# Biases as a weight row, casts and copies on ScalarE, maxima over two heads at once, in a fused transformer and mixture-of-experts kernel

## The chip, the cores and the metric

The kernel runs on one core of a Trainium2 chip. The metric is the time on the device, in microseconds, from the first to the last instruction of one launch, with what lies around it. TensorE does the matmuls and transposes, VectorE and ScalarE read their results out of PSUM, GpSimd does elementwise work in SBUF, and SyncE issues the DMAs.

## What is computed

The input is 32 sequences of 256 token ids. Width is 192, with 12 heads of 16.

1. An embedding with a position table and a layer norm.
2. Four layers of windowed attention and a feed-forward part, on 32 sequences of 256 tokens:

```
q, k, v = heads(h @ Wq + bq), heads(h @ Wk + bk), heads(h @ Wv + bv)
scores  = q k^T / sqrt(16), only for |i - j| <= 64 and unmasked keys, else -1e9
h = layer_norm(h + softmax(scores) v @ Wo + bo)
h = layer_norm(h + gelu(h @ W1 + b1) @ W2 + b2)
```

3. One causal layer: a layer norm, q/k/v with a bias from `b_attn`, rotary embedding of q and k, causal softmax attention, a projection, a second norm.
4. A mixture of experts on the second norm's result: a shared expert, sigmoid scores of 16 experts, each expert's choice of 1024 tokens, and their weighted outputs added.

## The kernel before, in words

Four parts run one after another: `embed`, `tower` (the four token layers, then the causal layer), `choose` (which tokens each expert takes) and `experts`. The change touches `tower` alone.

**Tiles.** A sequence is 256 tokens, two tiles of 128 partitions. Two sequences, the sets s = 0 and 1, are in flight. Each set has four PSUM banks of 128 x 512 f32, `bank[s][0..3]`. q and k are held as bf16 stacks `[hi, lo, ...]` (`stack`, six slices of 16 per head, padded to 128), so that a bf16 matmul of two stacks gives f32-like products; a DMA transposes the stacks into `qkT`.

**Halves.** Every engine walks the same list of halves (`token_layers` L1041, `causal_layer` L1060). In one half, four sequences at different stages are worked on, called G, V, F and K. G and F are of one set, V and K of the other:

- G: hidden states transposed (`pe_hidden_T`, L439), copied to `hTa` by ScalarE (L683), q/k matmuls (`pe_qk`, L446), bias added by VectorE (`dve_qk`, L782), in the causal layer the rotation (`rotary`, L803: tile 0 on GpSimd, tile 1 on VectorE), then the stack (`dve_stack`, L817).
- V: value matmuls (`pe_v`, L459), bias added by VectorE into `vaug` (`dve_v`, L792); SyncE issues the transposes of the stack.
- F: first pass of scores, for the row maxima (`pe_scores1`, L471, in banks 0 to 2 in turn; `dve_row_max`, L838, one head each); the maxima are rounded (`dve_maxima`, L850), transposed (`pe_maxima`, L487) and copied as extra rows of `qkT` (`dve_maxima_rows`, L860).
- K: second pass of scores (`pe_scores2`, L499), exponents by ScalarE (L673), products with the values (`pe_products`, L515), transposes back (L554), division (att, L887, in the token layers with L898), transposes of att (L435), projection (`pe_project`, L562), residual (L945) and norm giving h1 (token layers L768 and L778; causal layer L756 and L760 into `xr`), transposes of h1 (L435), up projection (L582, causal L612), activation, down projection (L594, causal L627), residual and second norm (token layers). The unkept keys' share (`pe_unkept`, L537) exists in the token layers alone.

There are 128 full halves in the token layers and 35 halves in the causal layer, of which 29 have both G and K.

**Order.** There is no scheduler: each engine's program order is the order in `tensor_half` (L632), `scalar_half` (L665), `vector_half` (L912) and `pool_half` (L1008), and semaphores hold an engine until what it needs is done. TensorE interleaves second-pass head i with first-pass head i - 4, with product groups after i = 6, 10 and 13, then runs the rest in a fixed row: hidden_T, unkept, output transposes, maxima, att_T, values, project, q/k, h1_T, up, down. VectorE runs: row maxima, `dve_maxima`, sums and division, maxima rows, values, residual and norm to h1, q/k, (causal: sigmoid and gated products, rotation of tile 1), stack, and last the residual and second norm. GpSimd in a causal half: residual plus bias and rstd of the input norm of F, rstd1 of K (L1022), then a wait for the first q/k tile of G and four rotation instructions (L807, L810, L813, L815). This is the last:

```python
            if K:
                s = K.s
                ph.wait(pool, "var1", s, K.it)
                ph.inc(nc.gpsimd.tensor_tensor(rstd[s][:], ve[s][:], half[:], ALU.pow), "rstd1", s)
            if G and causal:
                s = G.s
                ph.wait(pool, "qk", s, G.it, 1)
                rc = Chain(ph, pool, G, "rot")
                rotary(nc.gpsimd, rc.link, s, 0)
```

Of the kernel before, what the change touches and what calls it, by code (L numbers as in the profile page):

```python
# [26 lines left out]
P = 128  # L27
D = 192
# [30 lines left out]
TOK_STACK_LINKS = 3  # L59
# [286 lines left out]
def tower(nc, a, hbuf, am_d, xs, sd, out, B, L):  # L346
# [4 lines left out]
    with ExitStack() as ctx:  # L351
# [5 lines left out]
        bank = [[ctx.enter_context(nc.psum_tensor(f"bank{s}{i}", [P, 512], F32)) for i in range(4)] for s in ST]  # L357


        wqk = sb("wqk", [DC, 2, 2 * D], F32)  # L360
        wv = sb("wv", [DC, 2, D], F32)
# [3 lines left out]
        vqk = sb("vqk", [P, 2 * D], F32)  # L365
        vv = sb("vv", [P, D], F32)
# [18 lines left out]
        hTa = sbs("hTa", [DC, 2, S], F32)  # L385
# [9 lines left out]
        mx = sbs("mx", [P, T, NH], F32)  # L395
        mrow = sbs("mrow", [P, T, NH, 32], BF16)
# [23 lines left out]
            sc1=NH, mx=NH, m=1, mT_ps=3, mT=3, sc2=NH, p=NH, pv=NH, ot=1, otT_ps=2, att=1,  # L420
# [18 lines left out]
        def pe_hidden_T(ph, pe, G, F, causal):  # L439
            s = G.s  # L440
            if F:
                ph.wait(pe, "y" if causal else "r2", F.s, F.it, 0)
            ph.wait(pe, "x0" if causal else "h_in", s, G.it)
            ph.inc(pe_transposes((h1 if causal else hcur)[s], bank[s][3]), "hT_ps", s)

        def pe_qk(ph, pe, G, F):  # L446
# [6 lines left out]
            for t in range(T):  # L453
                for c in range(2):
                    last = nc.tensor.matmul(bank[s][t][:, 0:2 * D], hTa[s][:, c, t * P:(t + 1) * P],  # L455
                                            wqk[:, c, :], start=(c == 0), stop=(c == 1))
                ph.inc(last, "qk_ps", s)

        def pe_v(ph, pe, V, G):  # L459
# [5 lines left out]
            for t in range(T):  # L465
                for c in range(2):
                    last = nc.tensor.matmul(bank[1 - s][3][:, t * D:(t + 1) * D], hTa[s][:, c, t * P:(t + 1) * P],
                                            wv[:, c, :], start=(c == 0), stop=(c == 1))
            ph.inc(last, "v_ps", s)

        def pe_scores1(ph, pe, F, h, masks, qcols, causal):  # L471
# [6 lines left out]
            if h >= 3:  # L478
                ph.wait(pe, "mx", s, F.it, h - 2)
            dst = bank[s][h % 3]  # L480
# [6 lines left out]
        def pe_maxima(ph, pe, F):  # L487
# [3 lines left out]
            for f in range(3):  # L491
                dst = bank[s][f][:].bitcast(BF16)
# [6 lines left out]
        def pe_scores2(ph, pe, K, V, h, masks, kcols):  # L499

            s = K.s
            if h == 0 and V:
                ph.wait(pe, "qk", V.s, V.it)
            if h == 0:
# [10 lines left out]
        def pe_products(ph, pe, K, F, g, kcols):  # L515
# [4 lines left out]
            if g == 2 and F:  # L520
                ph.wait(pe, "v", F.s, F.it)
# [110 lines left out]
        def tensor_half(ph, pe, G, V, F, K):  # L632
            causal = ph is not tok
            qcols, kcols, masks = (CAUSAL_Q, CAUSAL_K, 2) if causal else (BAND_COLS, BAND_COLS, 0)
            for i in range(NH + LEAD):
                if K and i < NH:
                    pe_scores2(ph, pe, K, V, i, masks, kcols)
                if F and i >= LEAD:
                    pe_scores1(ph, pe, F, i - LEAD, masks, qcols, causal)
                if K and i in PLAN.prod:  # L640
                    pe_products(ph, pe, K, F, PLAN.prod.index(i), kcols)
# [22 lines left out]

# [1136 lines left out]
```

## Time and profile before

| | us |
|---|---|
| median of 3 runs | 7051.08 |
| lowest, highest | 7049.91, 7069.48 |
| the profiled execution | 7050.01 |
| its span | 7048.2 |
| TensorE busy | 6042.4 (86% of the span) |
| VectorE busy | 4250.6 (60%) |
| ScalarE busy | 2239.1 (32%) |
| GpSimd busy | 1101.6 (16%) |

The mean granted TensorE clock is 0.939 of full speed; it has two levels, 2.4 GHz (1.0) and 1.2 GHz (0.5). Lines such as L435 are lines of the kernel before. "Idle before, releaser" is time in which an engine did nothing ahead of the instruction and what ended it. The chain of work that ended last covers only the last part of the span, the experts, so it says nothing about the changed part. To read the changed part, one has to look at the waits and at one half in order of time.

### The profile page before, as it was taken

What the parts mean: (1) busy time and instruction counts of PE and PEld (TensorE: products, weight loads), DVE (VectorE), ACT (ScalarE), POOL (GpSimd) and SP (SyncE); (2) the same over time, 40 slices, a digit from 0 to 9 for tenths busy, and PEclk for the clock granted to TensorE, in tenths of its full rate; (3) what the DMA queues carried; (4) which work ended last, traced back from release to release, by engine and by line L of the source; (5) the groups of instructions that cost most, each with busy time, mean ns of one, the idle gap of its engine ahead of it and who ended that gap; (6) DMA issues with size and microseconds to landing.
All of it is one profiled execution on the core that took longest, in us unless ns stands there. A gap on an engine that the chain in (4) does not pass through costs nothing. (4 is left out here: it accounts for less than half of the span.)

```text
span 7048.2 us, 128877 instructions
## 1 busy us (share of the span) xinstructions
PE 6042.4 (86%) x46786; PEld 4744.2 (67%) x46786; DVE 4250.6 (60%) x11172; ACT 2239.1 (32%) x4196; POOL 1101.6 (16%) x1089
## 2 busy tenths in 40 slices
PE   1999999999999999999999999978888883289999
PEld 0777777777777777777777777756666662266766
DVE  6666666666666666666666666666666664722222
ACT  0333333333333333334333333323333330011111
POOL 5011111111111111111111111111111110234333
PEclk9999999999999999999999999989999986699999
DMA  6322223323232322222332232332222320033322
GB/s 119 62 60 60 60 61 65 70 61 66 58 64 60 75 61 60 60 60 60 67 70 61 62 65 60 65 69 56 62 64 63 64 56 10 1 84 73 88 69 55
DMA packets 1204450, 441.09 MB, mean 63 GB/s; under 512 B 1050338, under 2 KB 1191044, under 8 KB 1204324
## 3 DMA queue, kind: packets, MB, share of 16 engines
q1 hardware_dynamic: 1176676, 402.69, 26.7%
q0 software_dynamic: 27648, 36.72, 3.4%
q8 instruction: 79, 1.29, 0.1%
q14 instruction: 47, 0.39, 0.0%
HBM read 124.23 MB, written 60.26 MB: 26 GB/s over the span
## 5 line engine op out<-in xcount | busy, mean ns | idle before, releaser
L673 ACT ACTIVATE pT<-bank 128x384 f32<-128x384 f32 x1920 | 907.9, 490 | 872.8 <-PE bank L511 872.8
L843 DVE TENSOR_REDUCE mx<-bank 128x2 f32<-128x384 f32 x1548 | 802.2, 554 | 322.0 <-PE bank L483 285.1
L582 PE MATMUL bank<-hT,w 96*128 96x256 f32 x3072 | 848.0, 442 | 85.9 <-ACT hT L688 85.9
L582 PEld LDWEIGHTS bank<-hT,w 96*128 96x128 f32 x3072 | 678.6, 224 | 236.2 <-ACT hT L688 118.2
L509 PE MATMUL bank<-maskb,eyeb 128*128 128x384 bf16 x1920 | 635.1, 331 | 78.6 <-ACT pT L673 73.3
L481 PE MATMUL bank<-maskb,eyeb 128*128 128x384 bf16 x1932 | 634.5, 328 | 39.9 <-DMA qkT<-stack 20.7
L483 PE MATMUL bank<-qkT 128*128 128x192 bf16 (+2 forms) x3864 | 636.5, 247 | 0.0
L511 PE MATMUL bank<-qkT 128*128 128x192 bf16 (+2 forms) x3840 | 630.9, 246 | 0.0
L993 DVE TENSOR_TENSOR hout<-bank,resid 128x384 f32<-128x384 f32 x128 | 71.3, 557 | 769.4 <-PE bank L594 769.4
L594 PE MATMUL bank<-w,pT 128*128 128x192 f32 x3072 | 520.4, 326 | 0.0
L1022 POOL TENSOR_TENSOR rstd<-ve,half 128x2 f32<-128x2 f32 x160 | 127.7, 798 | 2486.6 <-DVE ve L749 2486.6
L594 PEld LDWEIGHTS bank<-w,pT 128*128 128x128 f32 x3072 | 506.5, 190 | 6.6
L511 PEld LDWEIGHTS bank<-qkT 128*128 128x128 bf16 x3840 | 376.7, 98 | 136.9 <-issue 0.5
L483 PEld LDWEIGHTS bank<-qkT 128*128 128x128 bf16 x3864 | 379.4, 98 | 127.4 <-issue 2.2
L1709 PE MATMUL ps_g<-exp_xT,exp_wg 64*128 64x512 f32 x1152 | 456.6, 600 | 3.8 <-issue 3.1
L1709 PE MATMUL ps_u<-exp_xT,exp_wu 64*128 64x512 f32 x1152 | 446.7, 592 | 8.6 <-DMA emb_emb<-in_emb_word,emb_ids 7.3
L455 PE MATMUL bank<-wqk,hTa 96*128 96x384 f32 x1304 | 452.3, 490 | 1.4 <-ACT hTa L683 1.4
L531 PE MATMUL bank<-pT,vaug 128*32 128x192 f32 (+3 forms) x10752 | 413.5, 284 | 0.6 <-ACT pT L673 0.6
L688 ACT COPY hT<-bank 96x512 f32<-96x512 f32 x160 | 93.1, 582 | 1009.5 <-PE bank L435 1009.5
L701 ACT ACTIVATE pT<-bank,b 128x256 f32<-128x256 f32 x768 | 317.7, 472 | 294.1 <-PE bank L582 292.6
L1653 DVE TENSOR_TENSOR exp_hid<-exp_sg,ps_u 128x512 f32<-128x512 f32 x192 | 132.0, 687 | 429.5 <-PE ps_u L1709 368.5
L531 PEld LDWEIGHTS bank<-pT,vaug 128*32 128x32 f32 x10752 | 284.2, 109 | 117.6 <-issue 75.3
(197 smaller groups left out, 10230.5 us busy)
## 6 DMA issues: line engine op xcount, KB each, us to landing
hcur<-hbuf SPq DMA_DIRECT2D x165, 192.0 KB, 2.4
hbuf<-hout SPq DMA_DIRECT2D x128, 192.0 KB, 2.0
amb<-am_d SPq DMA_DIRECT2D x131, 128.0 KB, 2.9
exp_wg<-in_ewg SPq DMA_DIRECT2D x16, 768.0 KB
exp_wu<-in_ewu SPq DMA_DIRECT2D x16, 768.0 KB
exp_wd<-in_ewd SPq DMA_DIRECT2D x16, 576.0 KB
xs<-xr SPq DMA_DIRECT2D x32, 272.0 KB, 2.2
hbuf<-emb_z SPq DMA_DIRECT2D x17, 384.0 KB
```

Source lines behind the costliest of these rows:

```text
L455: last = nc.tensor.matmul(bank[s][t][:, 0:2 * D], hTa[s][:, c, t * P:(t + 1) * P], wqk[:, c, :], start=(c == 0), stop=(c == 1))
L481: nc.tensor.matmul(dst[:, 0:SCOLS], eyeb[:], maskb[:, masks, :], start=True, stop=False)
L483: last = nc.tensor.matmul(dst[:, c0:c0 + w], qT[s][:, h, t * P:(t + 1) * P], kT[s][:, h, f0:f0 + w], start=False, stop=(t == T - 1))
L509: nc.tensor.matmul(dst[:, 0:SCOLS], eyeb[:], maskb[:, masks + 1, :], start=True, stop=False)
L511: last = nc.tensor.matmul(dst[:, c0:c0 + w], kT[s][:, h, t * P:(t + 1) * P], qT[s][:, h, f0:f0 + w], start=False, stop=(t == T - 1))
L531: last = nc.tensor.matmul(dst[32 * j:32 * j + 32, at + f0:at + f0 + w], vaug[s][:, t, 4 * g + j, :], pT[s][:, (4 * g + j) % NPT, c0:c0 + w ...
L582: last = nc.tensor.matmul(bank[s][f // 2][:, (f % 2) * S:(f % 2 + 1) * S], w1[:, c, f * P:(f + 1) * P], hT[s][:, c, :], start=(c == 0), st ...
L594: last = nc.tensor.matmul(bank[s][3][:, t * D:(t + 1) * D], flat_pT(s)[:, f * S + t * P:f * S + (t + 1) * P], w2[:, f, :], start=(f == 0), ...
L673: ph.inc(nc.scalar.activation(pT[s][:, h % NPT, :], bank[s][h % 2][:, 0:SCOLS], ACT.Exp, scale=SCALE), "p", s)
L701: ph.inc(nc.scalar.activation(flat_pT(s)[:, f * S:(f + 1) * S], bank[s][f // 2][:, (f % 2) * S:(f % 2 + 1) * S], ACT.Gelu, bias=b1[:, f:f ...
L843: last = nc.vector.tensor_reduce(mx[s][:, :, h], src[:, 0:SCOLS].rearrange("p (t k) -> p t k", t=T), AX, ALU.max)
L1709: last = nc.tensor.matmul(dst[k % 2][:], w[u][rows, c, f * P:(f + 1) * P], xT[rows, c, n0:n0 + HALF], start=start, stop=stop)
```

## The change

The biases of q, k and v become row 97 of the first weight chunk (`wqkv` gets a row of biases, `hTa` a row of ones), so the matmul adds them. The additions of biases on VectorE and the two broadcast loads of biases per layer go. ScalarE copies the values from PSUM to `vaug` (`act_v`); in the causal layer it copies q and k (`act_qk`); in the token layers it writes their bf16 top part straight into the stack (`act_top`), and VectorE subtracts that from PSUM to get the remainder (`dve_rest`), in place of an addition, a cast and a subtraction. The row maxima are taken over two heads in one instruction. The banks move: first-pass scores use banks 0 to 3 in turn, hidden_T and the values bank 0, q/k banks 1 and 2, the maxima rows banks 1 to 3; some waits move with them.

```diff
...
-        wqk = sb("wqk", [DC, 2, 2 * D], F32)
-        wv = sb("wv", [DC, 2, D], F32)
+        banks = [ctx.enter_context(nc.psum_tensor(f"banks{s}", [P, 4, 512], F32)) for s in ST]
+        bank = [[banks[s][:, i, :] for i in range(4)] for s in ST]
...
+        wqk = sb("wqk", [DC + 1, 2, 2 * D], F32)
+        wv = sb("wv", [DC + 1, 2, D], F32)
...
-        vqk = sb("vqk", [P, 2 * D], F32)
-        vv = sb("vv", [P, D], F32)
...
-        hTa = sbs("hTa", [DC, 2, S], F32)
+        hTa = sbs("hTa", [DC + 1, 2, S], F32)
...
+        rows_of = lambda c: slice(0, DC + 1 - c)
...
-            sc1=NH, mx=NH, m=1, mT_ps=3, mT=3, sc2=NH, p=NH, pv=NH, ot=1, otT_ps=2, att=1,
+            qh=2, sc1=NH, mx=NH // 2, m=1, mT_ps=3, mT=3, sc2=NH, p=NH, pv=NH, ot=1, otT_ps=2, att=1,
...
         def pe_hidden_T(ph, pe, G, F, causal):
...
-                ph.wait(pe, "y" if causal else "r2", F.s, F.it, 0)
+                ph.wait(pe, "mx", F.s, F.it, 5)
...
-            ph.inc(pe_transposes((h1 if causal else hcur)[s], bank[s][3]), "hT_ps", s)
+            ph.inc(pe_transposes((h1 if causal else hcur)[s], bank[s][0]), "hT_ps", s)
...
         def pe_qk(ph, pe, G, F):
...
-                    last = nc.tensor.matmul(bank[s][t][:, 0:2 * D], hTa[s][:, c, t * P:(t + 1) * P],
-                                            wqk[:, c, :], start=(c == 0), stop=(c == 1))
+                    last = nc.tensor.matmul(bank[s][1 + t][:, 0:2 * D], hTa[s][rows_of(c), c, t * P:(t + 1) * P],
+                                            wqk[rows_of(c), c, :], start=(c == 0), stop=(c == 1))
...
         def pe_v(ph, pe, V, G):
...
-                    last = nc.tensor.matmul(bank[1 - s][3][:, t * D:(t + 1) * D], hTa[s][:, c, t * P:(t + 1) * P],
-                                            wv[:, c, :], start=(c == 0), stop=(c == 1))
+                    last = nc.tensor.matmul(bank[1 - s][0][:, t * D:(t + 1) * D], hTa[s][rows_of(c), c, t * P:(t + 1) * P],
+                                            wv[rows_of(c), c, :], start=(c == 0), stop=(c == 1))
...
         def pe_scores1(ph, pe, F, h, masks, qcols, causal):
...
-            if h >= 3:
-                ph.wait(pe, "mx", s, F.it, h - 2)
-            dst = bank[s][h % 3]
+            if h == 3:
+                ph.wait(pe, "y" if causal else "r2", s, F.it, 0)
+            if h >= 4 and h % 2 == 0:
+                ph.wait(pe, "mx", s, F.it, h // 2 - 1)
+            dst = bank[s][h % 4]
...
-                dst = bank[s][f][:].bitcast(BF16)
+                dst = bank[s][1 + f][:].bitcast(BF16)
...
-        def pe_scores2(ph, pe, K, V, h, masks, kcols):
+        def pe_scores2(ph, pe, K, V, F, h, masks, kcols):
...
+            if h == 0 and F:
+                ph.wait(pe, "v", F.s, F.it)
...
-        def pe_products(ph, pe, K, F, g, kcols):
+        def pe_products(ph, pe, K, g, kcols):
...
-            if g == 2 and F:
-                ph.wait(pe, "v", F.s, F.it)
...
+        def act_v(ph, act, V, K, causal):
+            s = V.s
+            ph.wait(act, "v_ps", s, V.it)
+            if K:
+                ph.wait(act, "otT_ps", K.s, K.it)
+                if not causal:
+                    ph.wait(act, "u_ps", K.s, K.it)
+            ph.inc(nc.scalar.copy(vaug[s][:, :, :, 0:DH],
+                                  bank[1 - s][0][:, 0:2 * D].rearrange("p (t h d) -> p t h d", t=T, h=NH)), "v", s)
...
+        def act_top(ph, act, G):
...
+            s = G.s
+            ph.wait(act, "xp", s, G.it, 0)
+            for t in range(T):
+                ph.wait(act, "qk_ps", s, G.it, t + 1)
+                ph.inc(nc.scalar.copy(stack[s][:, t].rearrange("p s h (m d) -> p (s h) m d", d=DH)[:, :, 0, :],
+                                      bank[s][1 + t][:, 0:2 * D].rearrange("p (x d) -> p x d", d=DH)), "qh", s)
...
+        def act_qk(ph, act, G):
+            s = G.s
+            for t in range(T):
+                ph.wait(act, "qk_ps", s, G.it, t + 1)
+                ph.inc(nc.scalar.copy(qk[s][:, t].rearrange("p s h d -> p (s h d)"), bank[s][1 + t][:, 0:2 * D]), "qk", s)
...
         def scalar_half(ph, act, G, V, F, K):
...
-                ph.inc(nc.scalar.copy(hTa[G.s][:], bank[G.s][3][0:DC, :]), "hT", G.s)
+                ph.inc(nc.scalar.copy(hTa[G.s][0:DC], bank[G.s][0][0:DC, :]), "hT", G.s)
...
+            if V:
+                act_v(ph, act, V, K, causal)
+            if G:
+                (act_qk if causal else act_top)(ph, act, G)
+            if K:
...
-        def dve_qk(ph, dve, G):
+        def dve_rest(ph, dve, G):
...
-            if G.wqk is not None:
-                dve.wait_ge(w_qk, G.wqk)
...
-                ph.wait(dve, "qk_ps", s, G.it, t + 1)
-                ph.inc(nc.vector.tensor_tensor(qk[s][:, t].rearrange("p s h d -> p (s h d)"),
-                                               bank[s][t][:, 0:2 * D], vqk[:], ALU.add), "qk", s)
...
-        def dve_v(ph, dve, V):
-            s = V.s
-            if V.wv is not None:
-                dve.wait_ge(w_v, V.wv)
-            ph.wait(dve, "v_ps", s, V.it)
-            ph.inc(nc.vector.tensor_tensor(
-                vaug[s][:, :, :, 0:DH],
-                bank[1 - s][3][:, 0:2 * D].rearrange("p (t h d) -> p t h d", t=T, h=NH),
-                vv[:].rearrange("p (h d) -> p h d", h=NH).unsqueeze(1).to_broadcast([P, T, NH, DH]),
-                ALU.add), "v", s)
+                ph.wait(dve, "qh", s, G.it, t + 1)
+                ph.inc(nc.vector.tensor_tensor(
+                    rem[s][:, t].rearrange("p s h d -> p (s h) d"),
+                    bank[s][1 + t][:, 0:2 * D].rearrange("p (x d) -> p x d", d=DH),
+                    stack[s][:, t].rearrange("p s h (m d) -> p (s h) m d", d=DH)[:, :, 0, :], ALU.subtract), "qk", s)
...
-        def dve_stack(ph, dve, ch, F, kbcol):
+        def dve_stack(ph, dve, ch, F, kbcol, split):
...
-            ph.wait(dve, "xp", s, F.it, 0)
-            ch.link(lambda: nc.vector.tensor_copy(sl(0), flat(qk[s])))
-            ch.link(lambda: nc.vector.tensor_tensor(flat(rem[s]), flat(qk[s]), sl(0), ALU.subtract))
+            if split:
+                ph.wait(dve, "xp", s, F.it, 0)
+                ch.link(lambda: nc.vector.tensor_copy(sl(0), flat(qk[s])))
+                ch.link(lambda: nc.vector.tensor_tensor(flat(rem[s]), flat(qk[s]), sl(0), ALU.subtract))
...
-        def dve_row_max(ph, dve, F, h, qcols):
+        def dve_row_max(ph, dve, F, p, qcols):
...
-            ph.wait(dve, "sc1", s, F.it, h + 1)
-            src = bank[s][h % 3]
+            ph.wait(dve, "sc1", s, F.it, 2 * p + 2)
+            src, at = banks[s][:, 2 * (p % 2):2 * (p % 2) + 2, :], slice(2 * p, 2 * p + 2)
...
-                last = nc.vector.tensor_reduce(mx[s][:, :, h], src[:, 0:SCOLS].rearrange("p (t k) -> p t k", t=T),
-                                               AX, ALU.max)
+                last = nc.vector.tensor_reduce(mx[s][:, :, at].rearrange("p t h -> p h t"),
+                                               src[:, :, 0:SCOLS].rearrange("p h (t k) -> p h t k", t=T), AX, ALU.max)
...
-                    last = nc.vector.tensor_reduce(mx[s][:, t, h:h + 1], src[:, c0:c0 + w], AX, ALU.max)
+                    last = nc.vector.tensor_reduce(mx[s][:, t, at], src[:, :, c0:c0 + w], AX, ALU.max)
...
         def dve_maxima_rows(ph, dve, F):
...
-                ph.inc(nc.vector.tensor_copy(qkT[F.s][DC:P, f * 4:f * 4 + 4, :], bank[F.s][f][DC:P, :].bitcast(BF16)),
+                ph.inc(nc.vector.tensor_copy(qkT[F.s][DC:P, f * 4:f * 4 + 4, :], bank[F.s][1 + f][DC:P, :].bitcast(BF16)),
...
-                for h in range(NH):
-                    dve_row_max(ph, dve, F, h, qcols)
-                    if causal and h == 7:
+                for p in range(NH // 2):
+                    dve_row_max(ph, dve, F, p, qcols)
+                    if causal and p == 3:
...
-                    if causal and h == 10:
+                    if causal and p == 4:
...
-            if V:
-                if K:
-                    ph.wait(dve, "otT_ps", K.s, K.it)
-                    if not causal:
-                        ph.wait(dve, "u_ps", K.s, K.it)
-                dve_v(ph, dve, V)
...
-            if G:
-                dve_qk(ph, dve, G)
+            if G and not causal:
+                dve_rest(ph, dve, G)
...
-                dve_stack(ph, dve, sc, G, kb[:, NT:NT + T] if causal else kb[:, bass.ds(G.pair * (NST * T) + s * T, T)])
+                dve_stack(ph, dve, sc, G, kb[:, NT:NT + T] if causal else kb[:, bass.ds(G.pair * (NST * T) + s * T, T)],
+                          causal)
...
+            for s in ST:
+                nc.vector.memset(hTa[s][DC:DC + 1], 1.0)
...
                 def load_qk(l):
...
-                    sp.dma_start(vqk[:], a["vec"][bass.ds(l, 1), 0:2 * D].to_broadcast([P, 2 * D])).then_inc(w_qk, 16)
...
                 def load_v(l):
...
-                    sp.dma_start(vv[:], a["vec"][bass.ds(l, 1), 2 * D:3 * D].to_broadcast([P, D])).then_inc(w_v, 16)
...
+    bqkv = vec[:, 0:3 * D]
+    biased = np.concatenate([chunks(wqkv, DC), np.stack([bqkv, np.zeros_like(bqkv)], 1)[:, None]], 1)
...
-        "wqkv": chunks(wqkv, DC), "wo": chunks(wo, DC), "w1": chunks(w1, DC), "w2": chunks(w2, P), "vec": vec,
+        "wqkv": biased, "wo": chunks(wo, DC), "w1": chunks(w1, DC), "w2": chunks(w2, P), "vec": vec,
...

```

## Rows read from the trace of the kernel before

**Rows 1.** By stage: stretch, length, busy us of five engines, clock, DMA, GB/s.

```profile
150.00:4640.00 4490.00, 4093.35 (x34156) 3300.21 (x34156) 2951.99 (x7743) 1705.92 (x3202) 465.32 (x513) 0.96 0.31 63
4640.00:5900.00 1260.00, 1044.04 (x7430) 775.20 (x7430) 800.89 (x2497) 397.86 (x768) 181.07 (x226) 0.89 0.28 60
```

**Rows 2.** TensorE waits, token stage: waiter, releaser, total us, times, longest.

```profile
PE bank L435 <- DVE h L778: 127.1, 126, 1.1
PE bank L435 <- DVE att L898: 95.9, 126, 0.8
```

**Rows 3.** Waits of TensorE, causal stage, 28 halves.

```profile
PE bank L435 <- DVE xr L760: 34.7, 28, 1.3
PE bank L435 <- DVE h L756: 32.9, 29, 1.2
...
PE bank L481 <- DVE mx L847: 13.1, 28, 0.5
```

**Rows 4.** VectorE timeline, one token half: start, length, work, idle before.

```profile
3012.51 1.49 DVE L843 TENSOR_REDUCE mx<-bank 128x2 f32<-128x384 f32 x3 [1.00 <-PE bank L483]
...
3017.24 0.38 DVE L875 TENSOR_SCALAR den<-bank,amc 128x12 f32<-128x12 f32 x2 [1.06 <-PE bank L554]
...
3022.53 0.56 DVE L945 TENSOR_TENSOR h<-bank,resid 128x384 f32<-128x384 f32 x1 [0.65 <-PE bank L569]
...
3024.21 0.74 DVE L768 SCALAR_TENSOR_TENSOR h<-h,mv,vec 128x192 f32<-128x192 f32 x2
```

**Rows 5.** Timeline of weight loads, same token half.

```profile
3014.43 0.43 PEld L435 LDWEIGHTS bank<-eye,hcur 128*96 128x96 f32 x4
```

**Rows 6.** Groups by shape, 150:4800 us: busy, mean ns, idle before.

```profile
L843 DVE TENSOR_REDUCE mx<-bank 128x2 f32<-128x384 f32 x1548 | 802.2, 554 | 322.0 <-PE bank L483 285.1
L673 ACT ACTIVATE pT<-bank 128x384 f32<-128x384 f32 x1572 | 743.6, 490 | 732.0 <-PE bank L511 732.0
...
L569 PE MATMUL bank<-wo,hT 96*128 96x192 f32 x1048 | 191.7, 326 | 0.0
L544 PE MATMUL bank<-vaug,wam 128*128 128x192 f32 x1024 | 187.6, 326 | 0.0
...
L826 DVE TENSOR_TENSOR rem<-qk,stack 128x768 f32<-128x768 f32 x136 | 130.3, 958 | 4.7
```

**Rows 7.** Timeline of GpSimd, same token half.

```profile
3024.38 0.81 POOL L1022 TENSOR_TENSOR rstd<-ve,half 128x2 f32<-128x2 f32 x1 [16.38 <-DVE ve L749]
```

**Rows 8.** Timeline of TensorE, one causal half.

```profile
5236.79 1.78 PE L455 MATMUL bank<-wqk,hTa 96*128 96x384 f32 x5
5239.77 0.64 PE L435 MATMUL bank<-eye,xr 128*96 128x128 f32 x4 [1.20 <-DVE xr L760]
```

**Rows 9.** Timeline of GpSimd, same causal half.

```profile
5237.87 0.70 POOL L1022 TENSOR_TENSOR rstd<-ve,half 128x2 f32<-128x2 f32 x1 [9.32 <-DVE ve L749]
5240.26 0.60 POOL L807 TENSOR_TENSOR rem<-qk,rope 128x192 f32<-128x192 f32 x1 [1.69 <-DVE qk L789]
5240.94 0.60 POOL L810 TENSOR_TENSOR rem<-qk,rope 128x192 f32<-128x192 f32 x1
```

**Rows 10.** Timeline of VectorE, same causal half.

```profile
5238.60 0.67 DVE L756 TENSOR_SCALAR xr<-hout,mv,rstd 128x192 f32<-128x192 f32 x2 [0.81 <-POOL rstd L1022]
5239.18 0.53 DVE L760 TENSOR_SCALAR xr<-hout,mv,rstd 128x64 f32<-128x64 f32 x2
...
5242.54 0.18 DVE L963 TENSOR_SCALAR sig<-sig 128x32 f32<-128x32 f32 x1 [1.90 <-ACT sig L691]
```

**Rows 11.** Timeline of VectorE, the causal half before it.

```profile
5205.86 0.76 DVE L963 TENSOR_SCALAR sig<-sig 128x32 f32<-128x32 f32 x1 [2.31 <-ACT sig L691]
```

**Rows 12.** Timeline of GpSimd, at the same moment.

```profile
5205.59 0.99 POOL L815 TENSOR_TENSOR qk<-qk,rem 128x384 f32<-128x384 f32 x1
```

**Rows 13.** Busy time by half, from one hTa copy to the next.

```profile
3015.15:3048.57 33.42, 30.62 (x268) 24.85 (x267) 22.85 (x61) 13.25 (x26) 3.61 (x4) 1.00 0.31 63
...
3085.45:3120.56 35.11, 32.30 (x268) 26.04 (x267) 22.85 (x61) 13.36 (x26) 3.62 (x4) 0.95 0.29 60
```

More of the change, by code:

```diff
@@ L56 @@
 SCOLS = 384
-TOK_STACK_LINKS = 3
+TOK_STACK_LINKS = 1
 CAUSAL_STACK_LINKS = 7
@@ L354, in tower @@
         sem = Semaphores(nc)
-        bank = [[ctx.enter_context(nc.psum_tensor(f"bank{s}{i}", [P, 512], F32)) for i in range(4)] for s in ST]
-        wqk = sb("wqk", [DC, 2, 2 * D], F32)
-        wv = sb("wv", [DC, 2, D], F32)
+        banks = [ctx.enter_context(nc.psum_tensor(f"banks{s}", [P, 4, 512], F32)) for s in ST]
+        bank = [[banks[s][:, i, :] for i in range(4)] for s in ST]
+        wqk = sb("wqk", [DC + 1, 2, 2 * D], F32)
+        wv = sb("wv", [DC + 1, 2, D], F32)
         wo = sb("wo", [DC, 2, D], F32)
@@ L636, in tensor_half @@
                 if K and i < NH:
-                    pe_scores2(ph, pe, K, V, i, masks, kcols)
+                    pe_scores2(ph, pe, K, V, F, i, masks, kcols)
                 if F and i >= LEAD:
@@ L640, in tensor_half @@
                 if K and i in PLAN.prod:
-                    pe_products(ph, pe, K, F, PLAN.prod.index(i), kcols)
+                    pe_products(ph, pe, K, PLAN.prod.index(i), kcols)
             if G:
@@ L1037, in turn @@
         def turn(s, it, pair, layer):
-            return Turn(s, it, pair, (layer + 1) * 32, (layer + 1) * 32, (layer + 1) * 16, (layer + 1) * 80)
+            return Turn(s, it, pair, (layer + 1) * 16, (layer + 1) * 16, (layer + 1) * 16, (layer + 1) * 80)
         def token_layers(eng, half_of):
@@ L1209, in _ @@
                     load_back(l + 1)
-                sp.wait_ge(w_qk, 32 * (L + 1))
-                sp.wait_ge(w_v, 32 * (L + 1))
+                sp.wait_ge(w_qk, 16 * (L + 1))
+                sp.wait_ge(w_v, 16 * (L + 1))
                 sp.wait_ge(w_bo, 16 * (L + 1))
```

## The prediction

> **What bounds the kernel now.** I split the span by stage first [rows 1]. Two stages run the changed code: the token stage (4490 us, TensorE busy 4093) and the causal stage (1260 us, TensorE busy 1044); the other 1298 us aren't touched. VectorE is busy for 66% and 64% of them, so its busy time as such isn't the limit. TensorE's waits tell which VectorE work counts: in a token half 1.0 us for h1 and 0.76 for att [rows 2], in a causal half 1.2 for h1 (written into xr) and 1.1 for x0, with 0.5 for a maximum [rows 3]. Last I read both halves in order of time [rows 4, 8 to 10]. A half is 33.4 us at a granted clock of 1.00 and 35.1 where the clock fell for a part of it [rows 13]. An edit gains time only if it shortens what ends one of these waits.
>
> **The change part by part.**
>
> The bias row: a matmul over 97 rows instead of 96. 128 rows and 96 rows by 192 columns both take 326 ns [rows 6], so it costs 0. The DMAs that go (two broadcasts per layer) are on no wait: 0.
>
> The values go from VectorE (about 0.56 us) to ScalarE. After it VectorE already waited 0.65 us for the projection [rows 4], and the h1 chain starts there, so the gain is 0. On ScalarE a 384-column instruction takes 490 ns [rows 6]; it is busy 1706 of 4490 us, and the three new ones lie between the aT and the h1T copy. The last, behind the second q/k matmul group, has to end before h1 is transposed: that group ends 1.0 to 1.2 us ahead of the transposes [rows 2, 3], the copy takes 0.5. Cost 0; without that cover it would be 0.5 us per half.
>
> Top halves and remainder (token stage): two additions become two subtractions of like size, and a cast of 0.56 and a subtraction of 0.96 us [rows 6] go. They stand behind h1 and ahead of a long wait for the down projection: 0 in steady state. Only at the two starts, where nothing overlaps, does the shorter chain show: 0.56 + 0.96 = 1.5 us each, -3 us.
>
> Maxima by pairs: 384 columns take 554 ns; 768 take 958, by the subtraction of that size [rows 6]. Six replace twelve, so VectorE saves about 0.9 us per half, in its waits for scores. What can be late is the bank that hidden_T now takes: it waits for pair 4. In the token half pair 3 is ready at 3012.51 [rows 4]; two pairs at a pitch of 0.863 (0.958 less the overlap of 0.095 seen between single ones: three take 1.49) end at 3014.33, and the weight load stands at 3014.43 [rows 5], after some 0.06 for the semaphore. Slack 0.04: I take 0, bounds 0 and +0.15 us, which over 128 halves is 0 to +19. The last maximum comes 0.4 later, but VectorE then idled 1.06 before the sums [rows 4]: 0. Bank 3 now waits for r2 at first-pass score 3, which has eleven score groups of the same half and one product group ahead of it on TensorE, each over 0.3 us: 0. In the causal half the 0.5 us wait for a maximum goes, but x0 was waited for behind it anyway, and the last pair (0.95) replaces the last head (0.55 [rows 6]), which pushes the maxima rows: estimate +0.15, bounds -0.25 and +0.4 us, times 29 halves that have both G and K: +4 (-7 to +12).
>
> **The rotation starts earlier**, and here I expect the cost. GpSimd's queue in a causal half is: rstd1, then wait for q/k of tile 0, then four rotation instructions. Before, that wait was for VectorE, whose addition stood behind all of h1: the rotation began 1.69 us after rstd1 [rows 9]. Now ScalarE copies tile 0 as soon as its four matmuls are done (the fourth starts at 5236.79 and it and four more take 1.78 [rows 8], so it ends by 5237.3; with 0.5 for the copy that is 5237.8). That is before rstd1 ends at 5238.57 [rows 9]. So rotation follows rstd1 directly, in the same moment as VectorE's two L756 and two L760, which write h1 (5238.60 to 5239.71 [rows 10]) and for which TensorE sits idle [rows 8].
>
> What such a meeting costs is in the trace: the 32-column tensor_scalar at L963 took 0.76 us and ended at 5206.62, 0.04 after GpSimd's L815 [rows 11, 12]; alone it took 0.18 [rows 10]. It was held until the GpSimd instruction ended. The Trainium skill (SBUF — State Buffer, Who interferes with whom) says that a tensor_scalar in a 2-port mode and a GpSimd instruction exclude each other for the whole instruction, and whoever issues first gets the ports; the hold at L963 agrees. By that rule alone, with GpSimd in turn after each VectorE instruction, the sum of this step would be the three GpSimd durations, 2.2 us per half, and 29 of them 64 us. L756 and L760 are tensor_scalar from SBUF to SBUF like L963, with 192 and 64 columns.
>
> Price: VectorE issues first (5238.60), its second L756 finds L807 (0.60) running, the third L810 (0.60) and the fourth L813 (1.0, as L815 [rows 12]). Held one by one that is 2.2 us less the 0.5 of gaps they fill: 1.7. The lower bound is one hold, 0.6; the upper is GpSimd first and four holds, 2.8. That GpSimd gets in between two VectorE instructions in a row I read from rstd1 in the token half: 0.81 us beside two L768 against 0.70 with VectorE idle [rows 4, 7, 9]; had it waited for both it would be 0.4 longer. I take 1.7, since holds alternated there. Nothing behind h1 gives it back: the transposes, the shared up projection and the exponents follow one after another. 29 x 1.7 = +49 us (17 to 81).
>
> **Sum**, from the profiled execution (7050.0 us, 1.1 below the median of the three): +49 +4 -3 +0 = +50, so 7100. About 0.3% (21 us) is what a measurement can tell from no change.
>
> **The rivals.**
> (a) *No collision that matters* (18%): VectorE's four instructions keep the ports, or rotation starts a little later. For it: they stand in a row without a wait. Against: the hold at L963. Time: 7050 +4 -3 = 7051.
> (b) *The pair's wait enters the token half* (10%, beside a collision of only one hold, +17): 128 x 0.15 = +19, giving 7050 + 19 + 17 + 1 = 7087. Against: slack of 0.04 computed.
> (c) *Faster by the clock* (7%): the granted clock dropped to 0.5 for part of many token halves. One such drop costs 35.11 - 33.42 = 1.69 us [rows 13]; a half with one of them has a mean clock of 0.95, and the whole token stage 0.96 [rows 1, 13], so there is about 0.8 of a drop per half, some 100 in 128 halves. A shift of the two waits by a tenth of a us can move drops in or out. It decides from 13 drops fewer (13 x 1.69 = 22 us) with no collision: 7051 - 24 = 7027 at 14. Against: the token half's waits stay as they are. The same mechanism can add as much.
> (d) *A worse clock in the causal half* (10%): the wait for h1 grows from 1.2 to some 3 us, and more halves get the longer drop; at an estimate of one more drop of 1.69 in every third half, 29 x 0.5 = +15 on top of the forecast: 7115. Against: the clock can also fall inside the wait, where it costs nothing.
>
> **How the numbers follow.** Forecast 55%, (a) 18, (b) 10, (c) 7, (d) 10. Slower holds the forecast but for its one-hold end (17 + 1 = 18 us, about 4%), (b) and (d), about 71%; same holds (a) but for 1% and the one-hold end, 21%; faster is (c) and 1% of (a), 8%. The range takes in (a) with the lower bound of the causal maxima (-7 in place of +4: 7040, cut to 7045 as only its rarest part), and at the top the forecast at 2.8 us of holds (7132) with the worse clock of (d) (+15): 7147, rounded to 7150. About 1 in 10 is left out below, (c), and 1 in 10 above and in the joint extremes. As cases of one sign hold most of the chance, it is one range.
>
> **What would show it.** Rotation (L807 on GpSimd) starts within 0.1 us of the end of rstd1, one or more of the four L756/L760 instructions of xr lasts 0.6 us or more longer, and TensorE's wait for xr grows from 1.2 to about 2.9 us; a token half stays at 33.4 us at full clock; the wait of scores for a maximum is gone; L825 and L826 are absent from the token stage. It is wrong if the xr instructions keep 0.67 and 0.53 us for two, or if hidden_T shows a wait for maxima in token halves.

## The result, and the profile after

| | before | after |
|---|---|---|
| median, us (4 runs each) | 7050.49 | 7141.18 |
| lowest to highest | 7048.53 to 7069.48 | 7134.49 to 7147.39 |
| ratio to before | | 1.0122 [1.0102, 1.0143] |
| span of the profiled execution | 7048.2 | 7132.7 |
| VectorE busy | 4250.6 | 3876.8 |
| ScalarE busy | 2239.1 | 2469.7 |

Slower by 1.2%. The change does what it says: VectorE has 374 us less to do and ScalarE 231 more. From here on a number such as L788 is a line of the changed kernel, and under an experiment a line of that experiment's own kernel. Groups by line, whole span (busy us, mean ns, idle before): a maximum over two heads takes 957 ns (958 was expected), a 384-column matmul over 97 rows 489.

```profile
L866 DVE TENSOR_REDUCE mx<-banks 128x4 f32<-128x768 f32 x774 | 729.5, 957 | 427.6 <-PE banks L485 424.5
L455 PE MATMUL banks<-wqk,hTa 97*128 97x384 f32 (+1 forms) x1304 | 453.1, 489 | 1.4 <-ACT hTa L710 1.4
```

**Where the 84.5 us of the span came from.** I counted halves from one copy of hTa to the next in the two traces. The first such copy is 8.2 us later (157.5 against 149.3), the first four halves take 2.0 us more, the next 126 take 2.1 less, the change of stage 2.4 more, the next 27 halves of the causal layer 68.6 more, all that follows 5.4 more. Those two long stretches, after (length, busy us of PE, PEld, DVE, ACT, POOL, clock, DMA share, GB/s):

```profile
240.11:4619.25 4379.14, 4007.71 (x33518) 3233.83 (x33517) 2556.82 (x6427) 1856.82 (x3529) 457.01 (x504) 0.97 0.31 62
4726.79:5787.18 1060.39, 887.16 (x6266) 667.76 (x6265) 630.00 (x1675) 374.30 (x729) 151.30 (x189) 0.89 0.27 58
```

The same 27 halves before:

```profile
4716.28:5708.09 991.81, 865.62 (x6266) 645.44 (x6265) 662.95 (x2080) 336.04 (x649) 150.88 (x189) 0.92 0.29 62
```

So the token stage takes the same time, though VectorE has 324 us less to do there, and a causal half went from 36.73 to 39.27 us. TensorE's waits, token stage and then causal stage (27 halves), after:

```profile
PE banks L435 <- DVE h L810: 125.7, 126, 1.1
PE banks L435 <- DVE att L921: 96.1, 126, 0.8
```

```profile
PE banks L435 <- DVE xr L792: 72.0, 27, 2.7
PE banks L435 <- DVE h L788: 41.0, 27, 1.5
...
PE banks L497 <- DVE mrow L880: 10.7, 27, 0.4
```

Against [rows 2] the first two are the same. Against [rows 3], the wait for xr went from 1.24 to 2.67 us a half (+1.43), that for x0 (the result of the input norm, which hidden_T transposes; here `h` of L788) from 1.13 to 1.52 (+0.39); the one for a maximum (0.47) went and one for the maxima rows (0.40) came. That is 1.75 of the 2.54 us. The rest is the 0.80 us a half that TensorE is busy longer (887.16 against 865.62 us in 27 halves) with the same number of instructions, at a granted clock of 0.89 instead of 0.92.

The timeline of one causal half shows the meeting (start, length, idle before):

```profile
5204.75 0.48 ACT L690 COPY qk<-banks 128x384 f32<-128x384 f32 x1 [2.04 <-PE banks L455]
...
5205.30 0.69 POOL L1040 TENSOR_TENSOR rstd<-ve,half 128x2 f32<-128x2 f32 x1 [9.06 <-DVE ve L781]
5205.96 0.60 POOL L828 TENSOR_TENSOR rem<-qk,rope 128x192 f32<-128x192 f32 x1
5206.03 1.32 DVE L788 TENSOR_SCALAR xr<-hout,mv,rstd 128x192 f32<-128x192 f32 x2 [0.81 <-POOL rstd L1040]
...
5206.64 0.60 POOL L831 TENSOR_TENSOR rem<-qk,rope 128x192 f32<-128x192 f32 x1
5207.27 1.30 DVE L792 TENSOR_SCALAR xr<-hout,mv,rstd 128x64 f32<-128x64 f32 x2
5207.31 0.99 POOL L834 TENSOR_TENSOR qk<-qk,rope 128x384 f32<-128x384 f32 x1
...
5208.64 1.07 PE L435 MATMUL banks<-eye,xr 128*96 128x128 f32 x4 [2.63 <-DVE xr L792]
```

ScalarE has q and k of tile 0 ready at 5205.23. rstd1 ends at 5205.99, the rotation (L828) has already been taken up by then (5205.96, where it was 1.69 us after rstd1 in [rows 9]), and the four instructions that write xr take 1.32 + 1.30 us in place of 0.67 + 0.53 [rows 10]. Taken singly (instructions of one line in that half; durations min/median/max, first and last start):

```profile
L788 DVE TENSOR_SCALAR xr<-hout,mv,rstd x2: 648/700/753, 5206.0 to 5206.6; 128x192 f32<-128x192 f32 x2
```

```profile
L792 DVE TENSOR_SCALAR xr<-hout,mv,rstd x2: 302/692/1082, 5207.3 to 5208.3; 128x64 f32<-128x64 f32 x2
```

The first three are held, by about 0.28, 0.38 and 0.78 us over the 0.37 and 0.30 that such instructions take at least in this stage, each until a GpSimd instruction has ended (5206.56, 5207.24, 5208.30); they end 0.12, 0.12 and 0.05 us behind it. All 27 halves show the same four durations within 5 ns. The fourth, from 5208.3, takes 0.30 and is free. The next transposes on TensorE last 1.07 us instead of 0.64 [rows 8], behind 2.63 us without work: in this half the granted clock falls to 0.5 as they start, at 5208.69.

### The profile page after: what moved, and what is told of

Read it like the earlier page. It is cut to its first block and busy times, and to the rows that moved or that the text cites. A ratio compares the mean times of both kernels' runs of the same rounds, so it can differ in the third digit from the quotient of the medians.

```text
span 7132.7 us, 126989 instructions
## 1 busy us (share of the span) xinstructions
PE 6062.9 (85%) x46786; PEld 4753.5 (67%) x46786; DVE 3876.8 (54%) x9528; ACT 2469.7 (35%) x4684; POOL 1103.0 (15%) x1089
## 5 line engine op out<-in xcount | busy, mean ns | idle before, releaser
L700 ACT ACTIVATE pT<-banks 128x384 f32<-128x384 f32 x1920 | 906.3, 489 | 860.1 <-PE banks L515 860.1
L866 DVE TENSOR_REDUCE mx<-banks 128x4 f32<-128x768 f32 x774 | 729.5, 957 | 427.6 <-PE banks L485 424.5
L584 PE MATMUL banks<-hT,w 96*128 96x256 f32 x3072 | 846.9, 442 | 85.8 <-ACT hT L720 85.8
L584 PEld LDWEIGHTS banks<-hT,w 96*128 96x128 f32 x3072 | 677.8, 224 | 235.9 <-ACT hT L720 118.2
L513 PE MATMUL banks<-maskb,eyeb 128*128 128x384 bf16 x1920 | 635.0, 331 | 79.9 <-ACT pT L700 74.0
L483 PE MATMUL banks<-maskb,eyeb 128*128 128x384 bf16 x1932 | 635.0, 329 | 27.8 <-DMA qkT<-stack 24.5
L485 PE MATMUL banks<-qkT 128*128 128x192 bf16 (+2 forms) x3864 | 637.4, 247 | 0.0
L515 PE MATMUL banks<-qkT 128*128 128x192 bf16 (+2 forms) x3840 | 630.9, 246 | 0.0
L596 PE MATMUL banks<-w,pT 128*128 128x192 f32 x3072 | 520.4, 326 | 0.0
L596 PEld LDWEIGHTS banks<-w,pT 128*128 128x128 f32 x3072 | 506.5, 190 | 6.6
L515 PEld LDWEIGHTS banks<-qkT 128*128 128x128 bf16 x3840 | 376.4, 98 | 136.7 <-issue 0.3
L485 PEld LDWEIGHTS banks<-qkT 128*128 128x128 bf16 x3864 | 379.8, 98 | 128.1 <-issue 2.9
L455 PE MATMUL banks<-wqk,hTa 97*128 97x384 f32 (+1 forms) x1304 | 453.1, 489 | 1.4 <-ACT hTa L710 1.4
```

Source lines behind the costliest of these rows:

```text
L455: last = nc.tensor.matmul(bank[s][1 + t][:, 0:2 * D], hTa[s][rows_of(c), c, t * P:(t + 1) * P], wqk[rows_of(c), c, :], start=(c == 0), sto ...
L483: nc.tensor.matmul(dst[:, 0:SCOLS], eyeb[:], maskb[:, masks, :], start=True, stop=False)
L485: last = nc.tensor.matmul(dst[:, c0:c0 + w], qT[s][:, h, t * P:(t + 1) * P], kT[s][:, h, f0:f0 + w], start=False, stop=(t == T - 1))
L513: nc.tensor.matmul(dst[:, 0:SCOLS], eyeb[:], maskb[:, masks + 1, :], start=True, stop=False)
L515: last = nc.tensor.matmul(dst[:, c0:c0 + w], kT[s][:, h, t * P:(t + 1) * P], qT[s][:, h, f0:f0 + w], start=False, stop=(t == T - 1))
L584: last = nc.tensor.matmul(bank[s][f // 2][:, (f % 2) * S:(f % 2 + 1) * S], w1[:, c, f * P:(f + 1) * P], hT[s][:, c, :], start=(c == 0), st ...
```

## The experiments

They ran on other chips than the pair above, where the kernel before takes 7012 to 7015 us, so I compare each by its ratio to the kernel before on the same chip and by its causal halves. Most of the gap to 7050 lies behind the tower: from its last matmul to the end it is 1169 us before and 1170 after, and 1139 to 1145 in the experiments. The changed kernel's own half is the same on both: 39.28 us in e2_split_load, where the tower differs in its loads alone. The 126 token halves, too, vary by up to 25 us with the same program: 4379 us in the changed kernel, 4355 in e6, which differs from it only in the causal part and the loads.

**Rotation held back until h1 is written** (e1_rot_after_h1), in `pool_half` of the changed kernel:

```diff
             if G and causal:
                 s = G.s
+                if K:
+                    ph.wait(pool, "h1", K.s, K.it)
                 ph.wait(pool, "qk", s, G.it, 1)
```

> The changed kernel with one wait more: in a causal half with both G and K, GpSimd waits for h1 before it starts the rotation of tile 0. ScalarE still copies q, k and the values at the same times. Theory (collision): the four xr instructions go back to 0.67 and 0.53 us for two, TensorE's wait for xr from 2.67 to about 1.24 us, and the kernel takes 29 x 1.43 = 41 us less, and up to 25 us less again where the granted clock stays up longer: 7075 to 7100. Rival 1 (ScalarE's new copies slow VectorE down): nothing moves, 7141. Rival 2 (what was lost sits in the maxima and the load at the start): less than 10 us gained.

Measured: 7001.85 us (10 runs), before 7012.13 (13 runs), ratio 0.9983 [0.997, 0.9997]. Its wait for xr in 26 halves of the causal stage, and the usual 27 halves:

```profile
PE banks L435 <- DVE xr L792: 32.1, 26, 1.3
```

```profile
4720.70:5683.97 963.27, 828.70 (x6266) 624.29 (x6265) 605.65 (x1675) 374.85 (x730) 150.89 (x189) 0.95 0.30 64
```

The wait for xr is back at 1.23 us and the causal half is 35.68: the whole loss in the causal stage is gone, and 1.06 us a half beyond it. ScalarE still makes its new copies, so rival 1 falls. By ratios the gain over the changed kernel is about 1.4%, some 95 us, where 41 to 66 were expected. 27 x 1.43 = 39 us of it are the wait. The other 2.2 us a half come with a clock of 0.95 instead of 0.89; that they are the clock's is shown only by the filled kernels below.

**The 97-row loads cut in two** (e2_split_load), in the changed kernel's weight loads:

```diff
-sp.dma_start(wqk[:], a["wqkv"][bass.ds(l, 1), :, :, 0:2 * D]...).then_inc(w_qk, 16)
+for r in (slice(0, DC), slice(DC, DC + 1)):
+    sp.dma_start(wqk[r], a["wqkv"][bass.ds(l, 1), r, :, 0:2 * D]...).then_inc(w_qk, 16)
```

and so for `wv`, with the counts that are waited for raised to 32.

> The changed kernel with the 97-partition weight loads split in two DMAs each: partitions 0 to 95 as before the change, and partition 96 alone. Theory (the 97-partition load runs on few DMA engines, so that the first q/k matmul starts 7 us late): the first matmuls go back to about 150 us from the start and the kernel takes 7 us less, about 7134; the causal half stays at 38.6 and 39.9 us. Rival (the late start is the memset of the row of ones, or chance in the embedding): no difference, 7141.

Measured: 7088.99 us, ratio 1.0107 [1.009, 1.0124], against 1.0122 [1.0102, 1.0143] for the changed kernel: 7 us are too few to be told apart in the whole time. The start shows them: the first copy of hTa comes at 150.87 instead of 157.5. It lies at 155.7 to 159.2 in all four kernels with the load of 97 partitions in one piece (after, e1, e3, e7) and at 147.9 to 151.2 in the five with it cut (e2, e5, e6, e8, e10). The changed kernel's stretches of 4 us ahead of the first half:

```profile
142.00:146.00 4.00, 0.00 (x0) 0.00 (x0) 3.43 (x9) 0.00 (x0) 0.00 (x0) 1.00 0.05 18
146.00:150.00 4.00, 0.00 (x0) 0.00 (x0) 3.19 (x16) 0.00 (x0) 0.00 (x0) 1.00 0.26 80
```

and SyncE's queue there, where the load of the hidden states stands behind that of the weights:

```profile
135.95 4.80 SPq L1165 DMA_DIRECT2D wqk<-in_wqkv  x1
140.79 7.14 SPq L1130 DMA_DIRECT2D hcur<-hbuf  x1
```

The same with the load cut in two:

```profile
142.00:146.00 4.00, 0.00 (x0) 0.00 (x0) 3.59 (x9) 0.00 (x0) 0.00 (x0) 1.00 0.84 249
146.00:150.00 4.00, 0.26 (x2) 0.25 (x3) 3.02 (x16) 0.00 (x0) 0.18 (x1) 1.00 0.85 219
```

```profile
135.66 5.72 SPq L1166 DMA_DIRECT2D wqk<-in_wqkv  x2
141.43 0.40 SPq L1130 DMA_DIRECT2D hcur<-hbuf  x1
```

In the stretch from 142 to 146 us the DMAs of the changed kernel move 18 GB/s at a share of 0.05, about one engine of sixteen, with the load of 97 partitions alone under way; the issue behind it takes 7.14 us instead of 0.40. With the load cut into 96 and 1 the stretch has 249 GB/s, which takes in the loads issued behind it too. The memset of the row of ones is the same in both, so that rival falls. The Trainium skill (DMA: Bandwidth & Descriptors, Why a DMA increments its semaphore by 16 and not by 1) says that a transfer is split over the largest number of engines, up to 16, that divides its slowest dimension: 97 is prime, so one. The share of 0.05 agrees.

**Maxima of one head again** (e3_single_max): in the changed kernel, `dve_row_max` over one bank, twelve times, with the waits of `pe_scores1` and `pe_hidden_T` recounted:

```diff
-            if h >= 4 and h % 2 == 0:
-                ph.wait(pe, "mx", s, F.it, h // 2 - 1)
+            if h >= 4:
+                ph.wait(pe, "mx", s, F.it, h - 3)
...
-                ph.wait(pe, "mx", F.s, F.it, 5)
+                ph.wait(pe, "mx", F.s, F.it, 9)
```

> The changed kernel with the row maxima over one head per instruction again, in the four banks of the change (score h waits for maximum h - 4, hidden_T for nine maxima), the input norm after heads 7 and 10 as before the change. Theory: the collision stays, so the xr wait stays at 2.67 us; in the causal half the wait for x0 falls from 1.52 to 1.1 or so and the 0.40 us wait for the rounded maxima goes, at no wait for maxima in the scores: about 0.5 us less in 29 halves, 15 us, some 7126. Token halves stay at 33.4 us. Rival (the pairing is what makes the causal half long): over 40 us less. Rival (pairing helps): slower than 7141 by 10 us or more.

Measured: 7095.07 us, ratio 1.012 [1.0103, 1.0136]; causal half 39.18, the 126 token halves 4369.7 us, within what they vary by. 0.09 us a causal half where 0.5 was expected: a miss. The wait for the maxima rows does go, but that for x0 grows to 1.8 us (29.1 us in 16 halves), and the wait for xr stays at 2.67 (45.4 in 17):

```profile
PE banks L435 <- DVE xr L792: 45.4, 17, 2.7
PE banks L435 <- DVE h L788: 29.1, 16, 1.9
```

So single heads give back next to nothing of what the causal half lost; the wait moves between x0 and the maxima rows.

**The kernel before with only the early copies** (e4_before_act_qk). Left out: the bias of q and k in the causal layer.

```diff
                 ph.inc(nc.scalar.copy(hT[s][:], bank[s][3][0:DC, :]), "aT", s)
+            if G and causal:
+                for t in range(T):
+                    ph.wait(act, "qk_ps", G.s, G.it, t + 1)
+                    ph.inc(nc.scalar.copy(qk[G.s][:, t]..., bank[G.s][t][:, 0:2 * D]), "qk", G.s)
...
-            if G:
+            if G and not causal:
                 dve_qk(ph, dve, G)
```

> The kernel before with one part of the change alone: in the causal layer ScalarE copies q and k out of PSUM in place of VectorE's addition. It leaves out the addition of the q and k biases in the causal layer. Theory (collision): rotation starts right behind rstd1 and the xr wait of TensorE grows from 1.24 to about 2.7 us; 29 x 1.43 = 41 us more and up to 25 us more by the clock: 7092 to 7117. Rival (the collision needs something else of the change): 7050.

Measured: 7087.03 us, ratio 1.0101 [1.0084, 1.0118]; causal half 38.82 (+2.09). Its wait for xr is 64.2 us in 24 halves, 2.68 each. VectorE, then GpSimd, in one causal half:

```profile
5229.61 1.32 DVE L761 TENSOR_SCALAR xr<-hout,mv,rstd 128x192 f32<-128x192 f32 x2 [0.81 <-POOL rstd L1027]
5230.85 1.30 DVE L765 TENSOR_SCALAR xr<-hout,mv,rstd 128x64 f32<-128x64 f32 x2
```

```profile
5228.88 0.69 POOL L1027 TENSOR_TENSOR rstd<-ve,half 128x2 f32<-128x2 f32 x1 [9.39 <-DVE ve L754]
5229.54 0.60 POOL L812 TENSOR_TENSOR rem<-qk,rope 128x192 f32<-128x192 f32 x1
```

This single part, put into the kernel before, brings the same 1.32 and 1.30 us and 1.0% of the 1.2%. Its waits for x0 (1.13 us) and for a maximum (0.47) stay as they were before.

**Both repairs together** (e5_rot_split: the edits of e1 and e2).

> The changed kernel with the rotation behind h1 and the weight loads split, both. If the two costs are separate, their gains add: ratio to the kernel before about 0.997 (rotation behind h1 alone gave 0.9983, and the split is 7 us, 0.1%). If the load's 7 us were hidden by something at the start, no gain over 0.9983.

Measured: 6980.77 us, before 7013.86 (8 runs), ratio 0.9952 [0.9935, 0.9968]; causal half 35.69, first copy at 150.65. That is a little better than the 0.997 expected. The profiled execution is 15 us shorter than that of e1: 5 us at the start, where the load is, 6 in the token halves, whose code is the same, and 3 behind the causal halves. So the two gains add, and what goes beyond the load's 0.1% lies elsewhere.

**And the input norm one pair of maxima earlier** (e6_rot_split_norm), for the wait for x0:

```diff
-                    if causal and p == 3:
+                    if causal and p == 2:
...
-                    if causal and p == 4:
+                    if causal and p == 3:
```

> The same, with the input norm in the causal half moved one pair of maxima earlier (begun after pair 2, ended after pair 3), into VectorE's wait of 1.18 us for pair 3. Theory (x0, not the maxima, holds hidden_T in the causal half): the 1.52 us wait for x0 falls to about 0.45 (then for pair 4), 1.0 us in 29 halves, 30 us: ratio about 0.993. Rival (the last pair of maxima holds TensorE anyway through the rounded maxima): the wait moves to the maxima rows, under 10 us gained.

Measured: 6956.65 us, ratio 0.9921 [0.9904, 0.9937], as expected (0.993); causal half 34.95, 0.74 less where 1.0 was expected, at a clock of 0.940 instead of 0.949. x0 is no longer waited for; the transposes now wait for the bank that pair 4 frees, 0.56 us a half (19 halves here):

```profile
PE banks L435 <- DVE mx L870: 10.6, 19, 0.7
```

**The clock apart from the waits** (e7_after_filled). To see what the collision costs with the clock held, I gave TensorE work whose result is overwritten in the stretches where it waits, in the changed kernel's causal stage: 15 matmuls before and 3 after the transposes of h1.

```diff
+        def pe_fill(dst, n):
+            for _ in range(n):
+                nc.tensor.matmul(dst[:, 0:SCOLS], eyeb[:], maskb[:, 0, :], start=True, stop=True)
...
             if K:
+                if G:
+                    pe_fill(bank[G.s][3], 15 if causal else 0)
                 pe_h1_T(ph, pe, K, xr if causal else h1)
+                if G:
+                    pe_fill(bank[G.s][3], 3 if causal else 0)
```

> The changed kernel, collision included, with TensorE kept busy in the causal half while it waits: 15 bf16 matmuls of 384 columns into a bank nobody reads, ahead of the transposes of h1 (0.16 us each, 2.4 us in a wait of 2.6), and 3 ahead of the up projection (0.5 in 0.67). Theory (the collision costs 1.43 us per half by itself, and the rest of the 2.5 us is the granted clock that falls after the longer wait): granted clock 1.00 through the causal stage, halves of 35.1 to 35.6 us in place of 39.3, some 105 us less than the changed kernel: ratio to before about 0.997. Rival (the clock falls for another reason): halves stay above 38 us.

Measured: 6990.37 us, ratio 0.9962 [0.9948, 0.9976]. The 27 halves, and one of them at full clock:

```profile
4719.95:5681.38 961.43, 866.73 (x6752) 639.77 (x6751) 631.40 (x1675) 374.87 (x730) 151.78 (x189) 0.99 0.30 64
```

```profile
5075.29:5110.64 35.35, 31.87 (x252) 23.48 (x251) 23.37 (x63) 13.90 (x28) 5.62 (x7) 1.00 0.30 64
```

VectorE still meets GpSimd as before (1.33 and 1.31 us for the instructions of xr), and TensorE does more, yet the causal half falls from 39.27 to 35.61 us on average and to 35.35 and 35.41 where the clock is 1.00: some 3.9 us of it were the clock. Ratio and half lie where the theory put them, and the rival falls.

**The fillers in all three kernels**: in the kernel before (e9_before_filled), in the one with both repairs (e10_rot_split_filled) and in that with the norm moved too (e8_all_filled). Token half: 4 before the transposes of att, 5 before and 3 after those of h1; causal half: 6 and 3. In e9 and e10 those around h1 write `bank[K.s][2]`, in e7 and e8 `bank[G.s][3]`.

> The kernel with rotation behind h1, split loads and the earlier norm, with such matmuls in the waits of both stages: in a token half 4 ahead of the transposes of att, 5 ahead of those of h1, 3 ahead of the up projection; in a causal half 6 and 3. Theory: the granted clock stays 1.00, token halves at 33.5 us in place of 34.8 on average (126 x 1.2 = 155 us) and causal halves at about 33 in place of 35.7: ratio about 0.965. Rival (idle time in these waits is not what drops the clock): no gain over the kernel with the earlier norm, or a loss of some 0.2 us per half where the matmuls end late.

> The kernel before the change with the same matmuls in its waits (4, 5 and 3 in a token half, 6 and 3 in a causal half). Theory (the clock is a matter of the waits alone): token halves at 33.4 and 33.6 us all through, causal halves at 33.7, ratio about 0.967. Rival (the clock gain needs the change): well above that.

> The changed kernel with rotation behind h1 and split loads, and the same matmuls; against the same kernel before, filled, it shows what the change itself is worth when the clock is equal. By the prediction's steps: token halves equal (0), causal halves +0.15 us (the maxima), the start -3: a difference of 0 to +5 us, within 0.1%. Rival (the change's savings on VectorE reach TensorE): 10 us or more below the filled kernel before. Without the earlier norm it should also be 25 to 35 us above the fully filled kernel, at a ratio of about 0.968.

| | us | ratio to before | causal half at full clock |
|---|---|---|---|
| before + fillers | 6785.62 | 0.967 [0.9657, 0.9683] | 33.75, 33.80 |
| repaired + fillers | 6801.58 | 0.9695 [0.9682, 0.9709] | 33.89, 33.95 |
| repaired, norm moved, + fillers | 6763.36 | 0.9639 [0.9623, 0.9655] | 32.84, 32.95 |

One half of each of the first two, and the 126 token halves of the third:

```profile
4905.96:4939.71 33.75, 30.57 (x243) 22.56 (x242) 24.37 (x78) 12.45 (x25) 5.58 (x7) 1.00 0.31 67
```

```profile
4841.38:4875.27 33.89, 30.40 (x243) 22.61 (x242) 22.64 (x63) 13.89 (x27) 5.60 (x7) 1.00 0.31 67
```

```profile
231.98:4463.38 4231.40, 4116.12 (x35030) 3264.63 (x35029) 2558.41 (x6427) 1854.31 (x3528) 457.30 (x504) 1.00 0.31 65
```

With the clock at 1.00, the 126 token halves take 4231.4 us here, 4233.9 in the kernel before and 4232.1 in the repaired one: the change is worth nothing there in either direction. In the causal half at full clock it costs 0.15 us (33.92 against 33.78), and moving the norm gives back 1.0. The fillers don't lengthen a half: those halves of e1, without fillers, whose clock is 1.00 take 33.9 to 34.0 us as well, and those of e6 32.8 to 32.9.

Two of the expectations were met (0.965 for e8 and 0.967 for e9), that of e10 was not: the repaired kernel with fillers is 16 us slower than the kernel before with them (0 to 5 expected), and 38 above e8 on another chip (25 to 35 expected). In the profiled executions, which differ by 7 us, the 27 causal halves are 10 us longer: four of them still take 35.4 to 35.6 us at a clock of 0.95, none of the kernel before does, and the means are 34.16 and 33.78. So the repaired change gains nothing even with the clock held up. The last kernel beats both the kernel before and the changed one; nearly all of that is the clock, which the kernel before takes as well.

## Why the prediction was right, and where its sizes were off

The forecast was 7100 us in a range of 7045 to 7150; the median is 7141. Direction, place and mechanism held; the excess over before was 91 us instead of 50. That the time still lies in the range is in part luck: the upper end was meant for holds of 2.8 us a half, and what filled it was the clock and a load at the start that the prediction had at nothing.

- **Bias row, matmul: 0.** Right: 489 ns against 490.
- **Bias row, loads: "on no wait".** Wrong for the load that grew. I priced the two broadcasts that go and not the weight load that went from 96 to 97 partitions. It cost 6.6 us at the first layer (e2), where nothing covers it.
- **Values to ScalarE, top halves, pairs in the token half: 0.** Right: 4379.1 against 4381.2 us for 126 halves, and no wait for maxima at hidden_T. VectorE's 324 us were never on TensorE's path. (The overlap of single maxima in [rows 4] is 0.086 and not 0.095, since three of 554 ns take 1.49 us; the slack is then 0.03, which changes nothing.) The 3 us expected at the starts don't show: with fillers and the loads cut, the first four halves take 80.1 us against 80.5 before. Rival (b) falls.
- **Pairs in the causal half, +0.15 (-0.25 to +0.4).** At full clock it is +0.15 (e9 against e10), which is all that the repaired change costs there. The wait that replaces the one removed was named as the maxima rows; x0's was not, and e3 shows that the two trade places.
- **The early rotation, 1.7 a half, +49.** The mechanism is shown from both sides: e4 adds it to the kernel before, e1 takes it out of the changed one. Its size was 1.43 us in the wait for xr; at full clock (35.38, the mean of 35.35 and 35.41, in e7, where the fillers lie inside the wait, less 33.92 in e10) it is 1.46, so 29 x 1.46 = 42 us. Three instructions are held, as forecast, but the first three and not the last three, since GpSimd's L828 was under way 0.07 us before VectorE's first: 0.28 + 0.38 + 0.78 = 1.44. So GpSimd was first, which the prediction had priced at its upper bound of 2.8 with a fourth hold; the fourth instruction started 0.11 us ahead of GpSimd's last and took its 0.30. The rule of the Trainium skill (SBUF — State Buffer, Who interferes with whom) agrees in that each hold ends with a GpSimd instruction; the 2.2 us that I worked out by it, the three GpSimd durations in full, is too high: a held instruction ends 0.05 to 0.12 us behind the GpSimd one, though alone it takes 0.30 to 0.37, so each hold covers 0.25 us of the instruction's own time, 0.75 us in all (2.2 - 1.44).
- **The clock, 0 in the sum and rival (d) at +0.5 a half.** This is the step that failed in size. At full clock, by the filled kernels, a changed half is 35.38 us and a half of before 33.78, 1.60 apart; measured they are 39.27 and 36.73. So the clock takes 3.9 us of the one and 2.95 of the other: +0.94 a half, 27 us in 29 halves. Rival (d), +0.5 a half, was right in kind and half the size, and could have been read as part of the forecast. Its argument against it, that the clock may fall inside the wait where it costs nothing, does not hold here: the transposes behind the wait take 1.07 us and TensorE is busy 0.80 us a half longer. Rivals (a) and (c) fall.

Sum as measured: 42 (collision) + 27 (clock) + 4 (pairs) + 7 (load) = 80, of 84.5 in the span. The clock's 27 is what the measured half leaves after the other two, and not a measurement of its own. The remaining 4.5 us are less than parts vary by that are not changed: the work behind the tower took 1138.5 to 1144.7 us in these experiments.

Left open: the repaired kernel without fillers has a causal half of 35.69 us against 36.73 before, though at full clock it is 0.15 slower. Its mean clock is 0.95 instead of 0.92, as the profile shows. Which of the smaller waits decides that was not tried. With fillers it was the other way about: there the kernel before kept its clock in all 27 halves and the repaired one did not.

## What to carry to other kernels

Before an operation is moved to an idle engine, look at what it was holding back: here the addition on VectorE kept GpSimd from starting, and the faster copy let it start on top of the four instructions that TensorE stood waiting for. An order that was an accident should be written down as a wait once its cause is moved. And count a TensorE wait together with the clock that follows it: 1.44 us more of waiting for xr cost 2.1 us a half when put into the kernel before (e4) and gave 3.6 when taken out of the changed one (e1), and TensorE work that nobody needs, put into the waits, gained 3.3% on the kernel before.

## What the runs showed of the hardware that was not expected

- A load of 97 partitions, alone under way, left the DMAs at 18 GB/s and a share of 0.05, and the issue behind it took 7.1 us; with 96 and 1 apart the same stretch moved 249 GB/s, and that issue took 0.40 us.
- With TensorE 86% busy over the whole run, waits of 1.0, 0.8 and 0.7 us in each token half of some 35 us come with a clock of 0.97 in the token stage; filled, it is 1.00 in all of it and 126 halves take 147 us less (4233.9 against 4381.2).
- GpSimd got its turn between two VectorE instructions that stood ready in a row, twice, after one that had started 0.07 us ahead of the first: xr's four took 2.5 us (5206.03 to 5208.58) instead of 1.1.
